# ScalarE takes the two exps of a slot ahead of the copy of its scores and of the row of maxima

## The chip, the cores and the metric

The kernel runs on one core of a Trainium2 chip. The metric is the device time in microseconds (us), the median of the runs. The engines are TensorE (PE in the profile, PEld for its weight loads), VectorE (DVE), ScalarE (ACT), GpSimd (POOL) and the queue that issues the DMAs (SP).

## The reference

A decoder layer with three parts, each added to x and followed by a layer norm: causal self-attention (32 heads of 16), cross-attention on a context of 1601 keys (32 query heads of 128, 8 key and value heads), and a mixture of 28 low-rank experts. Four batches of 256 rows of width 512. The change is in the cross-attention:

```python
q = (query @ Wq + bq).reshape(B, L, NKV, G, HDIM)
k_, v_ = jnp.split(kv @ Wkv + bkv, 2, axis=-1)
scores = jnp.einsum('blkgd,bmkd->bkglm', q, k) * scale
attn = jax.nn.softmax(scores, axis=-1)
o = jnp.einsum('bkglm,bmkd->blkgd', attn, v).reshape(B, L, NHEAD * HDIM)
return o @ Wo + bo
```

## The kernel before

The four batches run one after the other (b = 0 to 3). In each, self-attention comes first, then cross-attention, then the experts. Cross-attention is 32 heads (`NHB`; n counts them over all batches, 0 to 127). Values are held as a high and a low part, so each product is three matmuls.

**Slots.** The 1601 keys are 13 tiles of 128 (the last of 65), taken in pairs: `NSL` = 7 pairs a head, the seventh with one tile. Every engine runs the same loop, `for g in SLOTS`, and does in slot g what constants like `SCORE = -13` or `EXP = -3` say: a step with start t works at slot g on pair number g - t, counted through all heads of the batch. `slot_of` gives the (head, pair) of a step done for every pair; `head_of` that of a step done once a head. Nothing else sets the order: within a slot each engine's order is that of its code, and an engine waits at an instruction until its semaphores are there, with all behind it. Below, "slot s of head n" is the slot that weighs pair s of head n (`VALUE = 0`). In it run:

- PE: `scores` of the pair 13 further on (six matmuls into one of two banks; three where the pair is the short one, in slot 0), in slot 3 `spread_maxima` of the next head (L1151), in slot 6 `spread_reciprocals` (L1232), then the jobs of the slot, then `weigh` of pair s (six matmuls into dn; three in slot 6), in slot 1 `turn_maxima` of the next head (L1143), in slot 5 `sum_rows` (the matmuls sp<-cst,sua).
- ACT: in slot 0 `take_heads_sum` of the head just weighed (orw, L713), `keep_scores` (the copy kept_s from the scores' bank, L684, short form L682), in slot 3 `keep_max` of the next head (mrow, L692), `exponentials` of the pair 3 further on (ph, L702, into SBUF, and the same once more into a PSUM bank, sp, L705), then `job_high`, the high part of each job's result.
- DVE: `job_low` of the jobs of the slot before, `low_and_sum` of the pair 2 further on (pl, L904, and its sum: sua, L910, or L907, which for the first pair of a head starts the sum again), in slot 2 `row_maxima` (L893), in slot 5 `row_reciprocals` (L917), in slot 0 `normalize` (L924), then `maximum` of the pair 13 further on (mxa, L886, for the short pair L883).
- POOL: `shift_scores` of the pair 4 further on (L524, kept_s minus mrow), in slot 1 `finish_head` (L536 to L540); in the first batch also three splits of weight pieces a head (L514, L516), in slots 0, 2 and 4.

**Jobs** are the projections, in the two banks of a ring: for keys (K, twelve matmuls of 400 columns), queries (Q, twelve of 256), values (V, twelve of 256) and output (O, six of 512). Counted in a batch: heads 0 to 28 have a Q job in slot 2. Heads 7, 15, 23 have V jobs in slots 1 to 6, and the heads behind these (8, 16, 24) in slots 0 to 4. Heads 1, 5, ..., 25 have K jobs in slots 4 to 6 and heads 2, 6, ..., 26 one in slot 1. O jobs are in slots 3 and 5 of heads 3, 11, 19, 27; slots 5 and 6 of heads 4, 6, 12, 14, 20, 22, 28, 30; slots 1 and 3 of heads 9, 17, 25. So heads 0, 2, 10, 18, 26 and 29 have no job in slots 3 to 6.

**Waits that matter here.** `scores` waits for the copy (cp_ok) and the maximum (mx_ok) of the pair two before, which used its bank. The maximum waits for the copy (cp_ok). `shift_scores` waits for mrow (mr_ok) and the copy of its own pair, made nine slots earlier. The first exp waits for `shift_scores` (sb_ok) and for the weighing of the slot before (pv_mm), since ph has four places. The second also waits for DVE's sum in the slot before (su_ok), since its two banks are read there. L907 waits for `sum_rows` of the head before (sx_mm). `weigh` of a head's first pair waits for orw of the head before (oc_ok), since dn is one bank. `turn_maxima` waits for L883 (mx_ok).

Of the kernel before, what the change touches and what calls it, by code (L numbers as in the profile page):

```python
# [73 lines left out]
SCORE, SHIFT, EXP, LOW, VALUE = -13, -4, -3, -2, 0  # L74
# [4 lines left out]
def slot_of(g, start):  # L79

    h, s = divmod(g - start, NSL)
    return [(h, s)] if 0 <= h < NHB else []


def head_of(g, start):

    h, s = divmod(g - start, NSL)
    return [h] if s == 0 and 0 <= h < NHB else []
# [101 lines left out]
def build(nc, x, x_t, ctx_t, ws, wso, wk_in, wv_in, wq_in, wo_in, bo_s, bo_x, wb, wga, wlb, rope, consts, wk2, wv2, wq2, wo2, out, nb=B):  # L190
    with ExitStack() as ctx:
# [376 lines left out]
        def _(act):  # L568
# [18 lines left out]
            for b in range(nb):  # L587
# [63 lines left out]
                def job_high(kind, p, i):  # L651

                    act.wait_ge(job, jobs_to(b, kind, p, i))
                    src = ring_bank(b, kind, p, i)
                    done = (job_hi, 1)
                    if kind == "K":
                        kv, j = divmod(i, len(KCH))
                        a, n = KCH[j]
                        if b or p or kv:
                            act.wait_ge(sc_mm, (b * NHB + p * NHD + kv * G - 1) * NSL + last_slot_of(j) + 1)  # L660
                        nc.scalar.activation(kh[:, a:a + n], src[:, 0:n], ACT.Identity,
                                             bias=cst[:, 2 * p + C_BK + kv:2 * p + C_BK + kv + 1]).then_inc(*done)
                    elif kind == "Q":
                        h = p * NHD + i
                        if b * NHB + h >= G:
                            act.wait_ge(sc_mm, (b * NHB + h - G + 1) * NSL)
                        nc.scalar.activation(qh[:, h % G, :], src[:, 0:S], ACT.Identity,
                                             bias=cst[:, C_BQ + h:C_BQ + h + 1]).then_inc(*done)
                    elif kind == "V":
                        n = LAST if i == KT - 1 else P  # L670
                        if b or p:
                            act.wait_ge(pv_mm, (b * NHB + p * NHD - 1) * NSL + i // 2 + 1)
                        nc.scalar.activation(vh[0:n, i, :], src[0:n, 0:2 * P], ACT.Copy).then_inc(*done)

                def keep_scores(h, s):

                    n = b * NHB + h
                    k = n * NSL + s
                    src, dst = sbank[k % 2], kept_s[:, n % 2, 2 * s:2 * s + len(KEYS[s]), :].rearrange("p t q -> p (t q)")
                    act.wait_ge(sc_mm, k + 1)  # L680
                    if s == NSL - 1:
                        nc.scalar.activation(dst, src[:, 0:S], ACT.Identity, bias=cst[:, C_TAIL:C_TAIL + 1]).then_inc(cp_ok, 1)  # L682
                    else:
                        nc.scalar.activation(dst, src[:, :], ACT.Copy).then_inc(cp_ok, 1)  # L684

                def keep_max(h):

                    n = b * NHB + h
                    act.wait_ge(mr_mm, n + 1)
                    if n >= 2:  # L690
                        act.wait_ge(sb_ok, (n - 1) * NSL)
                    nc.scalar.activation(mrow[:, n % 2, :], mbank[:, 0:S], ACT.Copy).then_inc(mr_ok, 1)  # L692

                def exponentials(h, s):

                    n = b * NHB + h
                    k, cols = n * NSL + s, S * len(KEYS[s])
                    src = kept_s[:, n % 2, 2 * s:2 * s + len(KEYS[s]), :].rearrange("p t q -> p (t q)")
                    act.wait_ge(sb_ok, k + 1)
                    if k >= PH:  # L700
                        act.wait_ge(pv_mm, k - PH + 1)
                    nc.scalar.activation(ph[:, k % PH, 0:cols], src, ACT.Exp, scale=XSCALE).then_inc(ph_ok, 1)  # L702
                    if k >= 2:
                        act.wait_ge(su_ok, k - 1)
                    nc.scalar.activation(pbank[k % 2][:, 0:cols], src, ACT.Exp, scale=XSCALE).then_inc(pr_ok, 1)  # L705

                def take_heads_sum(h):

                    n = b * NHB + h
                    act.wait_ge(pv_mm, (n + 1) * NSL)  # L710
                    if n >= 2:
                        act.wait_ge(ot_ok, n)
                    nc.scalar.activation(orw[:, n % 2, :], dn[:, 0:S], ACT.Copy).then_inc(oc_ok, 1)  # L713
# [8 lines left out]
                for g in SLOTS:  # L722
                    for h in head_of(g, HEAD_SUM):
                        take_heads_sum(h)
                    for h, s in slot_of(g, SCORE):
                        keep_scores(h, s)
                    for h in head_of(g, MAX_ROW):
                        keep_max(h)
                    for h, s in slot_of(g, EXP):
                        exponentials(h, s)  # L730
                    for j in JOBS[g]:
                        if j[0] != "O":
                            job_high(*j)
# [620 lines left out]
```

## Time and profile before

| | us |
|---|---|
| median of 3 runs | 3050.05 |
| lowest, highest | 3045.78, 3051.54 |
| the profiled execution | 3042.88 |
| its span | 3041.1 |
| PE busy | 2831.5 (93%) |
| DVE busy | 2171.2 (71%) |
| ACT busy | 1906.0 (63%) |
| POOL busy | 1570.0 (52%) |

The numbers of one profile stand against its own time, 3042.88 us. A row of the time line has its start in us from the span's start, its duration in us, engine, line and operation, what it writes and reads, and in brackets the idle time of its engine ahead of it and what ended that. ACT's and DVE's operations overlap by about 0.1 us. A busy share is an average over stages with different limits. The cross-attention of the four batches lies at about 125 to 745, 890 to 1496, 1641 to 2247 and 2392 to 2998 us.

### The profile page before, as it was taken

How to read it: one execution, taken by the hardware profiler on the slowest of the kernel's cores; microseconds unless marked ns; L12 is line 12 of the kernel's file. 1: busy time of each engine (PE TensorE's matmuls, PEld its weight loads, DVE VectorE, ACT ScalarE, POOL GpSimd, SP SyncE). 2: the span in 40 equal slices, each digit the busy share in tenths (PEclk: the TensorE clock that was granted, in tenths of full speed). 3: DMA queues.
4: the chain of work that ended last, by engine and by line, in shares of the span. 5: the costliest groups of instructions: out<-in, count | busy, mean ns of one | idle time of the engine just before them, and what ended most of it. 6: DMA issues, size and time to landing. Idle time of an engine off the chain costs nothing.

```text
span 3041.1 us, 60253 instructions
## 1 busy us (share of the span) xinstructions
PE 2831.5 (93%) x20784; PEld 2619.2 (86%) x20784; DVE 2171.2 (71%) x4492; ACT 1906.0 (63%) x4264; POOL 1570.0 (52%) x1535
## 2 busy tenths in 40 slices
PE   7899999998899999999889999999978999999996
PEld 6789999997689999999668999999967899999985
DVE  5587777777558777777665877777756587878785
ACT  4476666665557666666565766666646576666663
POOL 4288787755125555555511645454542254555553
PEclk9999999998999999999899999999989999999998
DMA  5356564513311112121321112121222121212112
GB/s 186 134 190 208 165 215 162 178 50 115 103 42 56 70 64 77 63 77 63 121 89 43 65 62 77 64 77 56 80 111 89 36 84 42 97 43 91 50 53 97
DMA packets 97915, 285.08 MB, mean 94 GB/s; under 512 B 9936, under 2 KB 18256, under 8 KB 94416
## 3 DMA queue, kind: packets, MB, share of 16 engines
q1 hardware_dynamic: 97616, 281.24, 27.1%
q8 instruction: 170, 2.79, 0.4%
q14 instruction: 129, 1.06, 0.1%
HBM read 237.16 MB, written 44.04 MB: 92 GB/s over the span
## 4 chain that ended last, share of the span: by engine, by line
PE 78%; issue 7%; ACT 6%; POOL 3%; DVE 3%; DMA 2%; DVEq 0%; SPq 0%; ACTq 0%; POOLq 0%
PE bank L1012 41%; PE dn L1012 18%; PE sp L1012 14%; PE sp L1143 2%; ACT ph L702 2%; POOL kept_s L524 1%; ACT orw L713 1%; PE sp L1232 1%; PE sp L1083 1%; PE sp L1151 1%; ACT pn L629 1%; POOL lob L516 1%; DVE nmx L819 1%; POOL orw L536 0%; DMA wqk<-in_ws 0%
## 5 line engine op out<-in xcount | busy, mean ns | idle before, releaser
L524 POOL TENSOR_TENSOR kept_s<-kept_s,mrow 128x512 f32<-128x512 f32 (+1 forms) x896 | 1061.1, 1214 | 539.8 <-ACT mrow L692 539.8
L904 DVE TENSOR_TENSOR pl<-sp,ph 128x512 fp32r<-128x512 f32 (+1 forms) x896 | 577.0, 644 | 43.3 <-ACT sp L705 42.8
L702 ACT ACTIVATE ph<-kept_s 128x512 fp32r<-128x512 f32 (+1 forms) x896 | 534.8, 597 | 35.1 <-POOL kept_s L524 30.3
L1012 PE MATMUL dn<-ph,vh 128*128 128x256 f32 (+1 forms) x1664 | 492.5, 296 | 59.6 <-ACT orw L713 54.9
L705 ACT ACTIVATE sp<-kept_s 128x512 f32<-128x512 f32 (+1 forms) x896 | 506.3, 565 | 3.5 <-DVE sua L910 2.2
L910 DVE TENSOR_TENSOR sua<-sp,sua 128x512 f32<-128x512 f32 (+1 forms) x768 | 487.7, 635 | 0.0
L1012 PE MATMUL dn<-ph,vl 128*128 128x256 f32 (+1 forms) x1664 | 470.5, 283 | 0.0
L1012 PE MATMUL dn<-pl,vh 128*128 128x256 f32 (+1 forms) x1664 | 469.2, 282 | 0.0
L684 ACT ACTIVATE kept_s<-bank 128x512 f32<-128x512 f32 x384 | 229.0, 596 | 330.6 <-PE bank L1012 330.6
L1012 PEld LDWEIGHTS dn<-ph,vh 128*128 128x128 f32 (+1 forms) x1664 | 314.5, 189 | 95.2 <-ACT orw L713 86.6
L684 ACT ACTIVATE kept_s<-sp 128x512 f32<-128x512 f32 x384 | 229.6, 598 | 254.8 <-PE sp L1012 254.8
L536 POOL TENSOR_SCALAR orw<-orw,cst 128x256 f32<-128x256 f32 x128 | 118.3, 925 | 459.2 <-DVE orw L924 459.2
L1012 PEld LDWEIGHTS dn<-pl,vh 128*128 128x128 f32 (+1 forms) x1664 | 315.3, 189 | 5.6
L1012 PEld LDWEIGHTS dn<-ph,vl 128*128 128x128 f32 (+1 forms) x1664 | 315.3, 189 | 0.0
L1012 PE MATMUL bank<-wvx,ctxh 128*128 128x256 f32 (+1 forms) x1664 | 305.6, 282 | 0.0
L1012 PE MATMUL bank<-ctxh,wk 128*128 128x400 f32 (+1 forms) x1024 | 292.5, 348 | 3.1 <-DVE xres L843 3.1
L1012 PE MATMUL bank<-qh,kh 128*128 128x256 f32 (+1 forms) x832 | 245.2, 295 | 10.1 <-DVE ql L864 5.2
L1012 PEld LDWEIGHTS bank<-wvx,ctxh 128*128 128x128 f32 (+1 forms) x1664 | 251.2, 184 | 0.0
L907 DVE COPY sua<-sp 128x512 f32<-128x512 f32 x128 | 88.5, 691 | 223.8 <-PE sp L1012 223.8
L1012 PE MATMUL sp<-qh,kh 128*128 128x256 f32 (+1 forms) x832 | 243.2, 292 | 0.2
L1012 PE MATMUL bank<-wvx,ctxl 128*128 128x256 f32 (+1 forms) x832 | 233.7, 281 | 0.0
L1012 PE MATMUL sp<-qh,kl 128*128 128x256 f32 (+1 forms) x832 | 232.9, 280 | 0.0
(147 smaller groups left out, 7009.0 us busy)
## 6 DMA issues: line engine op xcount, KB each, us to landing
wqx<-wq SPq DMA_DIRECT2D x128, 512.0 KB, 3.4
wox<-wo SPq DMA_DIRECT2D x64, 1024.0 KB, 4.9
wk<-wk SPq DMA_DIRECT2D x32, 512.0 KB, 4.5
wvx<-wv SPq DMA_DIRECT2D x16, 1024.0 KB, 5.8
raw<-in_ctx_t SPq DMA_DIRECT2D x48, 200.0 KB, 2.5
wqk<-in_ws SPq DMA_DIRECT2D x17, 513.0 KB, 3.9
raw<-in_wq_in SPq DMA_DIRECT2D x32, 256.0 KB, 3.8
wq<-hib SPq DMA_DIRECT2D x32, 256.0 KB, 2.0
```

The source lines that it names most:

```text
L516: nc.gpsimd.tensor_tensor(lob[:, :], raw[:, r % 2, :], hib[:, :], ALU.subtract).then_inc(raw_free, 1)
L524: nc.gpsimd.tensor_tensor(kept_s[:, n % 2, i:z, :], kept_s[:, n % 2, i:z, :], mrow[:, n % 2, :].unsqueeze(1).broadcast_to([P, z - i, S]), ...
L536: nc.gpsimd.tensor_scalar(o, o, bias, None, ALU.add).then_inc(oh_ok, 1)
L629: nc.scalar.activation(pn[:, n % 3, a:z], s_bank[n % 5][:, a:z], ACT.Exp, bias=nmx[:, n % 3, qb:qb + 1], accum_out=sm[:, n % 3, qb:qb + 1] ...
L684: nc.scalar.activation(dst, src[:, :], ACT.Copy).then_inc(cp_ok, 1)
L702: nc.scalar.activation(ph[:, k % PH, 0:cols], src, ACT.Exp, scale=XSCALE).then_inc(ph_ok, 1)
L705: nc.scalar.activation(pbank[k % 2][:, 0:cols], src, ACT.Exp, scale=XSCALE).then_inc(pr_ok, 1)
L904: nc.vector.tensor_tensor(pl[:, k % PH, 0:cols], src, ph[:, k % PH, 0:cols], ALU.subtract).then_inc(pl_ok, 1)
L907: nc.vector.tensor_copy(sua[:, 0:cols], src).then_inc(su_ok, 1)
L910: nc.vector.tensor_tensor(sua[:, 0:cols], src, sua[:, 0:cols], ALU.add).then_inc(su_ok, 1)
L1012: return nc.tensor.matmul(dst, lhs, rhs, start=first, stop=final)
L1143: last = nc.tensor.transpose(mbank[:, col:col + P], mxa[:, e * S + tb * P:e * S + (tb + 1) * P], ident)
```

## The change

In ACT's loop the call of `exponentials` goes from behind `keep_scores` and `keep_max` to the place ahead of them. `take_heads_sum` stays first and `job_high` last.

```diff
                 for g in SLOTS:
                     for h in head_of(g, HEAD_SUM):
                         take_heads_sum(h)
+                    for h, s in slot_of(g, EXP):
+                        exponentials(h, s)
                     for h, s in slot_of(g, SCORE):
                         keep_scores(h, s)
                     for h in head_of(g, MAX_ROW):
                         keep_max(h)
-                    for h, s in slot_of(g, EXP):
-                        exponentials(h, s)
                     for j in JOBS[g]:
                         if j[0] != "O":
                             job_high(*j)
```

PE, DVE, POOL and SP keep their instructions in the same order; ACT has as many as before.

ACT, slots 3 to 5 of a head without a job there (head 2 of the first batch), before. The copies of the scores are kept_s, mrow is the row of maxima, ph and sp4<-kept_s are the two exps:

```order
L684 ACTIVATE kept_s<-bank2 128x512 [waits sc_mm]
L692 ACTIVATE mrow<-sp4 128x256 [waits sb_ok,mr_mm]
L702 ACTIVATE ph<-kept_s 128x256 [waits pv_mm,sb_ok]
L705 ACTIVATE sp4<-kept_s 128x256 [waits su_ok]
L684 ACTIVATE kept_s<-sp4 128x512 [waits sc_mm]
L702 ACTIVATE ph<-kept_s 128x512 [waits pv_mm,sb_ok]
L705 ACTIVATE sp4<-kept_s 128x512 [waits su_ok]
L684 ACTIVATE kept_s<-bank2 128x512 [waits sc_mm]
L702 ACTIVATE ph<-kept_s 128x512 [waits pv_mm,sb_ok]
L705 ACTIVATE sp4<-kept_s 128x512 [waits su_ok]
```

The same place in the changed kernel:

```order
L702 ACTIVATE ph<-kept_s 128x256 [waits pv_mm,sb_ok]
L705 ACTIVATE sp4<-kept_s 128x256 [waits su_ok]
L684 ACTIVATE kept_s<-bank2 128x512 [waits sc_mm]
L692 ACTIVATE mrow<-sp4 128x256 [waits sb_ok,mr_mm]
L702 ACTIVATE ph<-kept_s 128x512 [waits pv_mm,sb_ok]
L705 ACTIVATE sp4<-kept_s 128x512 [waits su_ok]
L684 ACTIVATE kept_s<-sp4 128x512 [waits sc_mm]
L702 ACTIVATE ph<-kept_s 128x512 [waits pv_mm,sb_ok]
L705 ACTIVATE sp4<-kept_s 128x512 [waits su_ok]
L684 ACTIVATE kept_s<-bank2 128x512 [waits sc_mm]
```

The short exps went ahead of mrow; the exps that need POOL's subtraction of mrow follow it directly, and the copy of slot 4 follows them.

ACT, slot 6 of the same head and slot 0 of the next, before (orw is the copy of the head's sum):

```order
L684 ACTIVATE kept_s<-sp4 128x512 [waits sc_mm]
L702 ACTIVATE ph<-kept_s 128x512 [waits pv_mm,sb_ok]
L705 ACTIVATE sp4<-kept_s 128x512 [waits su_ok]
L713 ACTIVATE orw<-dn 128x256 [waits ot_ok,pv_mm]
L682 ACTIVATE kept_s<-bank2,cst 128x256 [waits sc_mm]
```

And in the changed kernel:

```order
L702 ACTIVATE ph<-kept_s 128x512 [waits pv_mm,sb_ok]
L705 ACTIVATE sp4<-kept_s 128x512 [waits su_ok]
L684 ACTIVATE kept_s<-sp4 128x512 [waits sc_mm]
L713 ACTIVATE orw<-dn 128x256 [waits ot_ok,pv_mm]
L702 ACTIVATE ph<-kept_s 128x512 [waits pv_mm,sb_ok]
```

The copy now stands last ahead of orw, and the exps of slot 0 directly behind orw.

## Rows read from the trace of the kernel before

**Rows 1.** The page's first part: busy time, share of the span, instructions.

```profile
PE 2831.5 (93%) x20784; PEld 2619.2 (86%) x20784; DVE 2171.2 (71%) x4492; ACT 1906.0 (63%) x4264; POOL 1570.0 (52%) x1535
```

**Rows 2.** Busy us (instructions) of PE, PEld, DVE, ACT, POOL by stretch; clock; DMA.

```profile
1641.00:2247.00 606.00, 583.22 (x4446) 556.23 (x4444) 465.60 (x870) 405.05 (x841) 327.49 (x317) 1.00 0.20 70
```

**Rows 3.** Waits, whole span: who waited for whom, us in total, times, longest.

```profile
POOL kept_s L524 <- ACT mrow L692: 539.8, 118, 26.3
...
DVE sua L907 <- PE sp L1012: 223.8, 123, 3.2
...
PE dn L1012 <- ACT orw L713: 54.9, 85, 1.8
...
PE sp L1143 <- DVE mxa L883: 10.2, 33, 0.6
```

**Rows 4.** Time line of ACT, slots 3 and 4 of head 82 (head 18 of its batch).

```profile
2016.10 0.60 ACT L684 ACTIVATE kept_s<-bank 128x512 f32<-128x512 f32 x1 [0.83 <-PE bank L1012]
2016.60 0.38 ACT L692 ACTIVATE mrow<-sp 128x256 f32<-128x256 f32 x1
2016.86 0.42 ACT L702 ACTIVATE ph<-kept_s 128x256 fp32r<-128x256 f32 x1
2017.17 0.39 ACT L705 ACTIVATE sp<-kept_s 128x256 f32<-128x256 f32 x1
2017.74 0.60 ACT L684 ACTIVATE kept_s<-sp 128x512 f32<-128x512 f32 x1 [0.18 <-PE sp L1012]
2018.39 0.64 ACT L702 ACTIVATE ph<-kept_s 128x512 fp32r<-128x512 f32 x1
2018.93 0.58 ACT L705 ACTIVATE sp<-kept_s 128x512 f32<-128x512 f32 x1
```

**Rows 5.** Time line of POOL, the same place.

```profile
2017.05 3.79 POOL L524 TENSOR_TENSOR kept_s<-kept_s,mrow 128x512 f32<-128x512 f32 x3 [4.69 <-ACT mrow L692]
```

**Rows 6.** Time line of DVE and PE, head 82's slot 5 to head 83's slot 1.

```profile
2020.64 0.69 DVE L907 COPY sua<-sp 128x512 f32<-128x512 f32 x1 [0.41 <-PE sp L1012]
...
2025.24 0.41 DVE L883 TENSOR_TENSOR mxa<-bank,mxa 65x256 f32<-65x256 f32 x1
...
2025.70 0.55 PE L1143 MATMUL sp<-cst,mxa 128*128 128x128 f32 x3
```

**Rows 7.** Time line of all engines, change from head 80 to head 81.

```profile
1981.00 0.28 PE L1012 MATMUL dn<-pl,vh 128*128 128x256 f32 x1
1981.12 0.28 PE L1012 MATMUL dn<-ph,vl 128*128 128x256 f32 x1
...
1982.22 0.69 DVE L907 COPY sua<-sp 128x512 f32<-128x512 f32 x1 [1.37 <-PE sp L1012]
...
1983.53 0.62 ACT L702 ACTIVATE ph<-kept_s 128x512 fp32r<-128x512 f32 x1
...
1984.57 0.37 ACT L713 ACTIVATE orw<-dn 128x256 f32<-128x256 f32 x1
1984.69 0.68 DVE L886 TENSOR_TENSOR mxa<-sp,mxa 128x512 f32<-128x512 f32 x1
...
1985.00 0.38 PE L1012 MATMUL dn<-ph,vh 128*128 128x256 f32 x1 [0.78 <-ACT orw L713]
...
1986.82 0.41 DVE L883 TENSOR_TENSOR mxa<-bank,mxa 65x256 f32<-65x256 f32 x1
...
1988.63 0.60 PE L1143 MATMUL sp<-cst,mxa 128*128 128x128 f32 x4
```

**Rows 8.** Time line of ACT, slot 6 of head 2, first batch.

```profile
206.60 0.63 ACT L702 ACTIVATE ph<-kept_s 128x512 fp32r<-128x512 f32 x1 [0.75 <-POOL kept_s L524]
```

**Rows 9.** Time line of ACT, the first exp of the third batch.

```profile
1657.34 0.60 ACT L684 ACTIVATE kept_s<-bank 128x512 f32<-128x512 f32 x1 [0.33 <-PE bank L1012]
1657.96 1.28 ACT L702 ACT_TABLE_LOAD   x1
1659.25 0.64 ACT L702 ACTIVATE ph<-kept_s 128x512 fp32r<-128x512 f32 x1
```

## The prediction

> **What bounds the kernel now.** Read first the page's busy times and the table of windows [rows 1, 2]: TensorE (PE) is busy 93% of the span, and in the attention stretch of a later batch 583 of 606 us at full clock. So 1 us on PE's path is 1 us of the time, and what PE doesn't wait for is free. Then read the waits [rows 3]: the largest of PE's is for ScalarE's (ACT's) copy of a head's sum, orw L713: 54.9 us in 85 places. The second that matters here is for VectorE's (DVE's) last maximum of a head, mxa L883: 10.2 us in 33. The third thing to see there is GpSimd (POOL): it stands still 539.8 us until ACT has written mrow L692. At last read the time lines of two kinds of head [rows 4 to 7] and two single places [rows 8, 9].
>
> Slots are counted as in the text ahead: slot s of a head is the one that weighs its pair s.
>
> **What the change moves.** Nothing is added or taken out. ACT's exps go ahead of the copy and of mrow in every slot. The exps of slot g wait for POOL's subtraction, for the weighing of slot g-1 and (the second) for DVE's sum of slot g-1. The copy waits for the scores of slot g. The next operation starts 0.52 us after an exp and 0.50 us after a copy [rows 4, 7]. Two exps are 1.04 us against some 0.7 us from the end of a weighing to the end of the next scores (six matmuls, 0.12 us apart [rows 7]), so an undisturbed copy comes about 0.35 us later than now and the exps 0.7 us earlier. Who wants the copy? DVE's maximum, and the scores two slots on: 2.8 us or more later, so 0.35 us is hidden. Three places are left where it isn't so.
>
> **1. The slot after mrow (loss).** POOL can subtract only when mrow is there: in the head shown, mrow starts at 2016.60, POOL at 2017.05, and the first exp at 2018.39 [rows 4, 5]. Now the copy of slot 4 runs inside this wait, at 2017.74. Changed, it stands behind both exps: 2018.39 + 0.54 + 0.52 = 2019.45, which is 1.71 us later, and takes 0.60, to 2020.05. Does mrow itself move? Before it two exps of 256 columns now stand (0.31 us each, [rows 4]); they may start when the weighing of slot 2 ends and the 0.70 us of slot 3's scores cover their 0.62, so mrow stays where it is, by a margin of under 0.1 us.
> DVE takes the late copy first and then the rest in its fixed order: maximum 2020.08 to 2020.68, pl, and L907 from 2021.28 instead of 2020.64 [rows 6]. That is +0.64 us. PE's scores of slot 6 wait for that maximum (+0.3), the reciprocals' turn L1232 for DVE's L917 (+0.64). From L907 to L883 DVE has no gap: L907, L917, maximum, pl, sum, maximum, pl, sum, L924, L883. It ends now at 2025.65, PE's turn L1143 starts at 2025.70 [rows 6]: PE waits for it, so the 0.64 us reach the end of the kernel.
> Where does this hold? Where slots 3, 4 and 5 have no job for PE, so that DVE and PE are back at L907 before the delay is used up: heads 0, 2, 10, 18 and 26 of each batch. In the other heads an O, K or V job of 1.4 us or more (6 to 12 matmuls) lies between, and DVE waits for PE at L907 longer than 0.64 us. Head 29 has no job either, but DVE is behind there already: some 0.2 us. Sum: 5 x 0.62 + 0.2 = 3.3 us a batch; in the first batch POOL sets the pace around head 18 (below), and I take 2.7 + 0.5.
>
> **2. The change of heads (gain, mostly covered).** orw must be copied before PE may weigh the next head. Now it stands behind slot 6's copy and exps: in the second head shown the exps run from 1983.53 on, orw at 1984.57, PE goes on at 1985.00 after 0.78 us of waiting [rows 7]. Changed: the first exp at 1981.5, when the weighing that ends with the matmul at 1981.12 is done; the second waits for L907, which starts at 1982.22 and takes 0.69, so it runs at 1982.96; copy at 1983.48; orw at 1983.97. orw is 0.60 us earlier. (In the nearest simple count, the two exps gone from ahead of orw, it would be 0.66, down to the floor of the places where ACT isn't late.) There are 13 such places in a later batch and 8 in the first, each with the same 0.78 us.
> But what is late next? In 9 of 13 it is L883: the turn waits for DVE's gapless chain from L907, which is timed by PE's sums in slot 5 and not by orw. The first head shown is one: the turn starts 0.05 us after L883 ends [rows 6]. There the gain is 0. It remains where slot 1 has a job and DVE is done early: L883 at 1986.82, turn at 1988.63 [rows 7]. These are the changes into heads 9, 17 and 25, three a batch. Even there the next scores wait for the maximum that starts at 1984.69 [rows 7] and ends 0.68 later: 0.41 us of 0.60 are left. Gain 3 x 0.41 = 1.2 us a batch. The last place, in the batch's tail, is covered by DVE too.
>
> **3. Where POOL is late (loss).** In the first batch POOL splits the weights as well, and exps wait for it in front of orw: at 206.60 the exp of slot 6 starts after a wait of 0.75 us for POOL, and the copy has been made before it [rows 8]. Changed, the copy stands between exps and orw: +0.5 us on orw. These places are the changes into heads 1, 3, 11 and 19 to 21. The first three are heads of part 1, where the same 0.6 us of DVE's delay run beside this, so it isn't added; 19 to 21 are paced by POOL's own dense work, and 0.5 us is added once. That is the 0.5 above.
>
> **4. The table load.** ACT loads its table once a batch just ahead of the first exp, 1.28 us, and the exp starts 0.01 us after it ends [rows 9]. It now follows a copy that waited for PE; changed, it starts about 1 us earlier and falls into POOL's subtraction. What follows is timed by DVE: gain 0.1 us at most, taken as 0. The Trainium skill ("ScalarE: Activation LUTs", What ACT_TABLE_LOAD costs) gives the load 1283 ns, as here, and a drain of 1380 ns behind it. By that the chain would be some 0.4 us later a batch, an estimate from the page; the row shows no such drain.
>
> **The sum.** Later batches: 3.3 - 1.2 = +2.1 us each, 6.3 for three. First batch: 3.2 - 1.2 = +2.0. Together +8.3, taken as +8. The profiled execution took 3042.88 us (span 3041.1), so it would take 3050.9. It lies 7.2 us under the median of the runs shown, 3050.05; on that the forecast is **3058 us**, 0.26% slower. Bounds of my own sum: if each part-1 place costs 0.5 and the gain is the full 0.60, +4.5; if the gain is nothing and each place costs the 0.69 of a whole DVE instruction, +14.
>
> **Rivals.**
> A, the head changes pay in full (faster): if L883 isn't what the turn really waits for, or DVE's chain starts earlier with the exps, 47 places give 0.60 us: -28 us, 3022. For it speaks that orw is PE's largest wait [rows 3]; against it the 0.05 us between L883 and the turn. The Trainium skill ("Perfetto Trace Analysis", Optimization Strategies) advises to optimize the engines that keep matmuls waiting, which read on rows 3 is this rival; it says nothing of a second wait just behind.
> B, the two halves cancel (no change): DVE makes up the 0.64 us in part 1, say because pl or the maximum can run in the time in which it now waits for PE's sums. Then only the gain of 1.2 a batch is left: -5 to +4 us, 3045 to 3054. For it: DVE's waits for L907 are long in most heads (223.8 us in 123 places [rows 3]). Against: in the heads of part 1 there are just 0.4 us of it.
> C, mrow slips too (slower): the margin ahead of mrow is under 0.1 us. If the short exps aren't done when slot 3's scores are, mrow, POOL and the next exps slip by up to their 0.62 us in every head with few jobs. With some 22 such places on PE's path that is +14 on top: +22, 3072. It decides as soon as the weighing of slot 2 or DVE's sum of slot 2 ends later than now against the scores. The worst form of it is the first batch, where the exps ahead of mrow may wait for POOL, whose next work waits for mrow.
>
> **Chances.** Forecast 0.52, A 0.08, B 0.26, C 0.14. What a measurement can tell from no change is about 0.2%, 6.1 us; the forecast lies little above it, so of its 0.52 I give 0.36 to slower and 0.16 to the same. Slower 0.36 + 0.14 = 0.50, the same 0.16 + 0.26 = 0.42, faster 0.08. The range takes in B and the better part of C, and leaves A and C's worst out: 3044 to 3072.
>
> **What would show it.** In the changed kernel: (1) in heads 2, 10, 18, 26 and 0 the copy L684 of slot 4 starts some 1.06 us after an exp that waited for POOL, L907 no longer starts with the end of PE's sums but behind a pl, 0.6 us later, and these heads are longer by 0.6 us; (2) PE's wait for orw falls from 54.9 to about 25 us, while its wait for L883 grows from 10.2 by about as much as fell at the covered places; (3) heads 9, 17 and 25 begin 0.6 us earlier after their sums and keep 0.4; (4) POOL's start against mrow, and mrow against slot 3's scores, are unchanged. If mrow starts later than 0.5 us after the copy of slot 3 did, or if the copy of slot 3 waits behind short exps, C is at work. If L883 ends well ahead of the turn in heads 3 and 4, A is. The forecast falls as a whole if heads with jobs in slots 3 to 5 change their length too.

## The result

| | before | changed |
|---|---|---|
| median, us | 3050.05 | 3063.87 |
| lowest, highest | 3045.78, 3054.75 | 3063.12, 3067.60 |
| the profiled execution | 3042.88 | 3067.60 |
| its span | 3041.1 | 3065.8 |

The changed kernel takes 1.0049 times the time of before (95% interval 1.0034 to 1.0063), 10 to 19 us more. The forecast was 3058.0 us, range 3044 to 3072: slower, as forecast, and more than forecast. A second comparison of the same two kernels gave 1.0050 (1.0033 to 1.0067). Two executions in a slow state, one of 3960.02 us of the kernel with the change everywhere but in slot 4 and one of 6586.19 us of that with slot 6 alone, are in no median or ratio below.

The profile of the changed kernel answers to [rows 1] with this line: ScalarE (ACT) and VectorE (DVE) do the same instructions, TensorE (PE) is busy 25 us longer with the same 20784 matmuls.

```profile
PE 2856.9 (93%) x20784; PEld 2635.8 (86%) x20784; DVE 2154.2 (70%) x4492; ACT 1939.8 (63%) x4264; POOL 1571.4 (51%) x1535
```

Its waits, whole span (who waited for whom, us in total, times, longest), to be read against [rows 3]:

```profile
POOL kept_s L524 <- ACT mrow L692: 542.9, 124, 26.3
...
DVE mxa L886 <- ACT kept_s L684: 211.3, 160, 4.4
...
DVE sua L907 <- PE sp L1012: 193.0, 100, 3.2
...
PEld sp L1143 <- DVE mxa L883: 27.8, 56, 1.4
...
PE dn L1012 <- ACT orw L713: 22.8, 84, 1.5
...
PE sp L1143 <- DVE mxa L883: 15.0, 46, 1.2
...
PE sp L1232 <- DVE rs L917: 11.2, 32, 0.9
```

Several of them bear on the question. PE's wait for orw fell from 54.9 to 22.8 us, by 32 us. That didn't reach the end, and not all of it is orw being earlier: with the change in slot 4 alone, which leaves orw's place as it was, the wait falls to 46.6 us too (the two other profiles of the kernel before have 52.7), while PE waits longer at other places. DVE's wait for its copy grew from 46.1 to 211.3 us (most of it idle that costs nothing). PE's wait for L883 grew by 4.8 us, that of its weight loads (PEld) for the same L883 by 9.2 (18.6 before), and PE's for the reciprocals L917 by 5.9 (5.3 before). One more has no name. PE's own waits show it, here of the changed kernel; in the kernel before it is 4.3 us, 3 times:

```profile
PE bank L1012 <- issue: 19.2, 25, 1.4
```

**The slot after mrow.** The changed kernel's head 82 starts 13.71 us later than that of before (2021.20 against 2007.49). The time line from slot 3 to the turn in slot 1 of the next head, all engines, against [rows 4 to 6]:

```profile
2030.31 0.38 ACT L692 ACTIVATE mrow<-sp 128x256 f32<-128x256 f32 x1
...
2030.77 7.51 POOL L524 TENSOR_TENSOR kept_s<-kept_s,mrow 128x512 f32<-128x512 f32 x6 [4.69 <-ACT mrow L692]
...
2032.09 0.63 ACT L702 ACTIVATE ph<-kept_s 128x512 fp32r<-128x512 f32 x1 [1.40 <-POOL kept_s L524]
2032.62 0.58 ACT L705 ACTIVATE sp<-kept_s 128x512 f32<-128x512 f32 x1
2033.14 0.58 ACT L684 ACTIVATE kept_s<-sp 128x512 f32<-128x512 f32 x1
...
2033.76 0.69 DVE L886 TENSOR_TENSOR mxa<-sp,mxa 128x512 f32<-128x512 f32 x1 [1.91 <-ACT kept_s L684]
...
2034.96 0.68 DVE L907 COPY sua<-sp 128x512 f32<-128x512 f32 x1
...
2039.54 0.41 DVE L883 TENSOR_TENSOR mxa<-bank,mxa 65x256 f32<-65x256 f32 x1
...
2040.01 0.66 PE L1143 MATMUL sp<-cst,mxa 128*128 128x128 f32 x4 [0.17 <-DVE mxa L883]
```

Less 13.71, mrow and POOL stand at 2016.60 and 2017.06, where they were. The copy stands at 2019.43, which is 1.69 us later; L907 at 2021.25 (+0.61), L883 at 2025.83 (+0.59), the turn at 2026.30 (+0.60).

**A change of heads with orw early.** Head 80 to head 81, all engines, against [rows 7]; here the offset is 13.99 us:

```profile
1996.21 0.69 DVE L907 COPY sua<-sp 128x512 f32<-128x512 f32 x1 [1.49 <-PE sp L1012]
...
1996.94 0.60 ACT L705 ACTIVATE sp<-kept_s 128x512 f32<-128x512 f32 x1 [0.71 <-DVE sua L907]
...
1997.48 0.58 ACT L684 ACTIVATE kept_s<-sp 128x512 f32<-128x512 f32 x1
...
1997.96 0.37 ACT L713 ACTIVATE orw<-dn 128x256 f32<-128x256 f32 x1
...
1998.38 0.39 PE L1012 MATMUL dn<-ph,vh 128*128 128x256 f32 x1 [0.17 <-ACT orw L713]
...
1998.68 0.68 DVE L886 TENSOR_TENSOR mxa<-sp,mxa 128x512 f32<-128x512 f32 x1
...
1999.46 0.36 PE L1012 MATMUL sp<-qh,kh 128*128 128x256 f32 x1
```

Less 13.99, orw starts at 1983.97 and PE goes on at 1984.39, 0.61 earlier than before. The maximum L886 stays at 1984.69. The scores that wait for it start 0.10 us after its end, 0.34 earlier than before, and their first step is 0.20 us instead of 0.12: some 0.27 us are left.

**Where orw's 0.61 us goes to nothing.** Head 84 (local head 20), DVE and PE of the changed kernel:

```profile
2053.73 0.39 PE L1012 MATMUL dn<-ph,vh 128*128 128x256 f32 x1 [0.17 <-ACT orw L713]
...
2054.63 0.68 DVE L886 TENSOR_TENSOR mxa<-bank,mxa 128x512 f32<-128x512 f32 x1
...
2055.41 0.36 PE L1012 MATMUL bank<-qh,kh 128*128 128x256 f32 x1 [0.70 <-issue]
```

PE is let go by orw after 0.17 us, weighs, and stands 0.70 us in front of the scores, which start 0.10 us after the maximum L886 ends. The trace calls this wait "issue". In the kernel before, the same maximum starts at 2040.32, the scores at 2041.11: both have moved by 14.3 us. So the wait for orw became a wait for L886, at a place that the table of waits gives to nobody. That the scores start just behind L886, and wait for it in the code, is what names it; the trace itself gives no releaser, and no experiment moved L886 alone.

### The profile page after: what moved, and what is told of

It is laid out like the page before. It is cut to its first block, busy times and chain, and to the rows that moved or that the text cites. A ratio compares the mean times of both kernels' runs of the same rounds, so it can differ in the third digit from the quotient of the medians.

```text
span 3065.8 us, 60253 instructions
## 1 busy us (share of the span) xinstructions
PE 2856.9 (93%) x20784; PEld 2635.8 (86%) x20784; DVE 2154.2 (70%) x4492; ACT 1939.8 (63%) x4264; POOL 1571.4 (51%) x1535
## 4 chain that ended last, share of the span: by engine, by line
PE 67%; issue 14%; DVE 9%; POOL 4%; ACT 4%; DMA 1%; DVEq 0%; SPq 0%; ACTq 0%; POOLq 0%
PE bank L1012 36%; PE dn L1012 14%; PE sp L1012 11%; POOL kept_s L524 2%; DVE sua L910 2%; PE sp L1143 2%; DVE pl L904 1%; DVE mxa L886 1%; PE sp L1232 1%; PE sp L1083 1%; ACT pn L629 1%; PE sp L1151 1%; POOL orw L536 1%; DVE mxa L883 1%; ACT kept_s L684 1%
## 5 line engine op out<-in xcount | busy, mean ns | idle before, releaser
L1012 PE MATMUL dn<-ph,vh 128*128 128x256 f32 (+1 forms) x1664 | 495.5, 298 | 27.6 <-ACT orw L713 22.8
L1012 PE MATMUL bank<-qh,kh 128*128 128x256 f32 (+1 forms) x832 | 245.6, 295 | 20.4 <-issue 14.9
L886 DVE TENSOR_TENSOR mxa<-sp,mxa 128x512 f32<-128x512 f32 x256 | 174.2, 680 | 109.8 <-ACT kept_s L684 109.7
L886 DVE TENSOR_TENSOR mxa<-bank,mxa 128x512 f32<-128x512 f32 x256 | 174.1, 680 | 96.9 <-ACT kept_s L684 96.7
L1012 PE MATMUL sp<-ql,kh 128*128 128x256 f32 (+1 forms) x832 | 233.5, 281 | 0.0
```

What stands on the lines that cost most here:

```text
L886: nc.vector.tensor_tensor(mxa[:, 0:cols], sbank[k % 2][:, 0:cols], last, ALU.max).then_inc(mx_ok, 1)
L1012: return nc.tensor.matmul(dst, lhs, rhs, start=first, stop=final)
```

## The experiments

The kernels from here on have a condition for the place of `exponentials`; with `exps_first` always true it is the change. Only the condition is shown of each. The line numbers behind ScalarE's loop are 5 higher in these kernels, so L1148 is the turn that was L1143 and L888 the maximum that was L883.

```diff
+                    exps_first = g % NSL != 4
+                    if exps_first:
+                        for h, s in slot_of(g, EXP):
+                            exponentials(h, s)
                     for h, s in slot_of(g, SCORE):
                         keep_scores(h, s)
                     for h in head_of(g, MAX_ROW):
                         keep_max(h)
-                    for h, s in slot_of(g, EXP):
-                        exponentials(h, s)
+                    if not exps_first:
+                        for h, s in slot_of(g, EXP):
+                            exponentials(h, s)
```

"Heads 0 to 28" and "tail" (heads 29 and 30) below are the difference, from the starts of the heads' first weighing matmuls in two traces, between how long these heads last in a kernel and in the kernel before.

### Everywhere but in slot 4

> The change is kept in every slot but slot 4 (the one behind the row of maxima), which has the old order: copy, then exps. Theory 1 (the loss is the copy of slot 4, held behind exps that wait for POOL): the +0.60 us in slot 6 of heads 0, 2, 10, 18, 26 goes, five times a batch, and with it the three falls of the granted clock in the first batch (at 213, 370, 527 us of the changed kernel) and those in the tails of the later batches. What stays is the gain of some 0.3 us in heads 9, 17, 25: 3 to 8 us under the kernel before. Theory 2 (the later copy of every slot is to blame: DVE's wait for the copy is 211 us instead of 46): taking one slot in seven out gives back a seventh, so still 10 us or more slower than before.

Measured: 3055.02 us, 1.0017 (1.0005 to 1.0028). The expected loss of slot 4 is gone: heads 0 to 28 are 0.78, 0.51 and 0.89 us shorter in the three later batches. But the kernel isn't faster: the tail is longer by 2.7, 0 and 1.3 us, and the first batch by 4.1, where the clock falls at heads 1, 3, 11 and 19 (the runs of the kernel before, below, show that most of these 4.1 us come and go with the execution). The mechanism was there, its sign in the total was missed, and the falls, which were expected to go, stayed.

### Slot 4 alone

```diff
+                    exps_first = g % NSL == 4
```

> Only slot 4 has exps first, all other slots the old order. Theory 1: the losses without the gains: +0.6 us in heads 0, 2, 10, 18, 26 of each batch, PE's wait for orw about as before, 12 us or more slower than before, plus what the clock costs. Theory 2: a seventh of the change, so 2 us slower at most.

Measured: 3057.78 us, 1.0033 (1.0023 to 1.0044). Heads 0 to 28 are 2.95, 2.95 and 2.80 us longer in the later batches: 0.60 us for each of heads 0, 2, 10, 18 and 26, where it starts in slot 6, and nothing in the heads with jobs there. The waits show the place: the scores' maximum waits for the copy nearly as long as in the changed kernel, and PE for L917 at the turn of the reciprocals (L1237 here).

```profile
DVE mxa L891 <- ACT kept_s L684: 206.2, 152, 5.5
...
PE dn L1017 <- ACT orw L713: 46.6, 84, 1.8
...
PE sp L1237 <- DVE rs L922: 12.1, 34, 0.9
```

So the later copies of the other six slots add next to nothing to DVE's wait. The first batch is another matter: its heads 0 to 28 are only 0.59 us longer, against a profile of before that, like this one, has no fall of the clock in them. Heads 1, 3, 11 and 19 show none of the loss there. The two halves add: -0.78 + 2.95 = 2.17 in batch 1, and the changed kernel has 2.13.

### Slot 6 alone

```diff
+                    exps_first = g % NSL == 6
```

> Only slot 6 has exps first. Theory 1: orw 0.6 us earlier in 13 places a batch, of which only the changes into heads 9, 17, 25 keep some 0.3 us: 3 to 5 us faster than before in all, less 0.5 us at each of the places of the first batch where an exp waits for POOL in front of orw. Theory 3 (rival A of the prediction: the head changes pay in full once slot 4 is out of the way): 0.6 us at all 47 places, 20 us or more faster.

Measured: 3052.82 us, 1.0017 (1.0005 to 1.0028). Heads 0 to 28: -0.77, -0.80, -0.91. So the whole gain of the change comes from slot 6, and is 0.8 us in a later batch. PE's wait for orw is 26.9 us, and its nameless wait 15.5 us in 19 places, with no loss of slot 4 anywhere: it comes from orw being early. The tail is 1.3, 1.2 and 2.7 us longer, which makes it slower after all. 3 to 5 us faster had been expected. In the first batch slot 6 is a loss, not a gain. PE starts heads 1, 3, 11 and 19 later by about 0.5 us each, since the copy now stands between the late exps and orw:

```profile
213.86 0.39 PE L1017 MATMUL dn<-ph,vh 128*128 128x256 f32 x1 [2.13 <-ACT orw L713]
```

This is head 3; in the kernel before its wait is 1.64 us.

### Slot 6 alone, and DVE's maximum earlier

```diff
                 # DVE
+                    late_sum = g % NSL == 0
+                    if not late_sum:
+                        for h, s in slot_of(g, LOW):
+                            low_and_sum(h, s)
...
                         if s:
                             maximum(h, s)
+                    if late_sum:
+                        for h, s in slot_of(g, LOW):
+                            low_and_sum(h, s)
```

> Exps first in slot 6 alone, and in slot 0 DVE takes L924 and the maximum L883 ahead of pl and sua, so that L883 ends up to 1.2 us earlier. If the turn's wait for L883 is what covers the gain of the head changes, it now shows: the turn's waits (4.7 us a batch before) go, heads 3, 11, 19, 27 get 0.3 us or more from the earlier orw, and the kernel is 15 to 28 us faster than before. If the turn waits for something else, it is no faster than with slot 6 alone.

Measured: 3035.54 us, 0.9959 (0.9945 to 0.9974). With L883 moved forward, heads 0 to 28 of a later batch are 6.2 to 6.4 us shorter. The cover named in the prediction is real. The tails of the three later batches are 1.5 us longer each, with a fall of the clock. How much of the gain is DVE's alone, the next one tells.

### DVE's maximum earlier, ScalarE as before

```diff
+                    exps_first = False
```

(and DVE's order as in the last one)

> ScalarE's order as before; VectorE takes, in slot 0 of a head, the normalisation and the maximum L883 ahead of the low part and its sum (1.36 us earlier). Theory 1 (two waits one behind the other at the change of heads: orw first, L883 just behind): alone this pays only what TensorE's turn waits for L883 today, at most the 10.2 us of the wait in the trace of the kernel before, so 2 to 9 us faster. Together with the kernel that has the exps first in slot 6 alone (which was 5 us slower) the two edits would give 4 us faster at most if they simply added, and 14.5 us faster were measured for both in one kernel: theory 1 expects them not to add. Rival (the gain of that kernel came from VectorE's order alone): 14 us faster or more.

Measured: 3033.61 us, 0.9961 (0.9946 to 0.9977), 7 to 16 us faster. The bound of 10.2 us that was set for it is broken: heads 0 to 28 are 4.07, 4.09 and 4.16 us shorter, 12.3 us in the three batches, and some 3.5 in the first if the fall of the clock in head 3 is left out (that in head 19 is given back). The cause is a row that was read too narrowly. PE's wait for L883 is 10.2 us, but the turn's weight load waits for the same instruction, and that row of the kernel before is larger:

```profile
PEld sp L1143 <- DVE mxa L883: 18.6, 38, 0.8
```

With DVE's maximum early both rows are gone. Both edits together, in the kernel above, save 6.2 to 6.4 us a batch where they would give 0.8 + 4.1 = 4.9 if they only added. So about 1.3 us a batch of orw's gain had been behind L883. Even then only some 2.1 us of the 13 x 0.60 = 7.8 a batch come through; at heads 4, 12, 20 and 28 the maximum L886 still stops PE. The larger part of what the fourth kernel gained was DVE's own. The rival was nearer here than the theory. In the tails of the kernel with DVE's edit alone the turn no longer waits; PE has one idle stretch of 2.4 us at the spread of the maxima there, where the kernel before has two, of 0.6 and 1.6.

### The old order in the first batch

```diff
+                    exps_first = b > 0
```

> Exps first in the three later batches, the old order in the first. Theory 1 (the time is the sum of what the heads lose, place by place): the attention of the first batch lost 4.8 us in the changed kernel, of it 3.6 us behind falls of the granted clock in heads 3, 11 and 19; undone, the kernel is 8 to 11 us slower than before instead of 14, and no clock fall stands in those heads. Rival (falls of the clock there come with the run and not with the order): 13 to 15 us slower, falls in the first batch as before the undoing.

Measured: 3063.99 us, 1.0052 (1.0034 to 1.0071), no better than the changed kernel. The first batch has three falls of the granted clock, in heads 3, 11 and 19, though its order is the old one. The theory that the change makes them is out. In its profile the first batch's cross-attention is 3.3 us shorter than in the changed kernel (1.5 in heads 0 to 28, 1.8 in the tail), and the work ahead of it 2.2 us longer; that the medians show nothing of the 3.3 was not followed up.

### The old order in the last three heads

```diff
+                    exps_first = g < NSL * 29
```

> Exps first in heads 0 to 28 of each batch, the old order in the last three heads. Theory 1: the changed kernel lost 0.3, 1.9, 3.2 and 3.1 us in heads 29 and 30 of the four batches, because ScalarE's order there lengthens the idle stretches of TensorE and the granted clock halves; undone, about 8 us of the 14 come back: 4 to 8 us slower than before. Rival (a fall of the clock there comes with the run, since the kernel before has one in its first batch): 12 to 15 us slower.

Measured: 3061.17 us, 1.0044 (1.0027 to 1.0062), 13 us slower and so the rival's number. The tail is 0.0, 1.37, 1.36 and 1.34 us longer than in the profile of before instead of 0.3, 1.9, 3.2 and 3.1, which is 4.5 us less; 8 had been expected. What is left is a fall of the clock in head 30 in each batch.

### The kernel before, and the changed one, again

> The kernel before, once more. Theory 2 (falls of the granted clock behind the same idle stretches come with the run and not with ScalarE's order): the places inside the slots are the same to 0.02 us, but the falls stand elsewhere than at 726.6 us: some of heads 3, 11, 19 of the first batch and head 30 of any batch have one (1.5 and 1.4 us each) that had none, and the span is 2 to 8 us longer than 3041.1. Theory 1 (the order decides where they fall): falls at the same places, span within 1 us.

> The changed kernel, once more. Both theories: heads 0 to 28 of the later batches 2.0 to 2.5 us longer than in the kernel before. Theory 2: one or more of the seven falls in heads 3, 11, 19 of the first batch and head 30 of the four is missing or has another length. Theory 1: all seven again, with the lengths 3.4 us (first batch, second batch) and 6.8 us (last two).

Measured: before again, 3048.37 us, 0.9993 (0.9982 to 1.0005), span 3046.8; the changed one again, 3066.27 us, 1.0050 (1.0033 to 1.0067). In its later batches heads 0 to 28 of the kernel before last as long as in its first profile, to 0.2 us. In the first batch it now has falls in heads 3, 11 and 19 that the first profile had not, and one more at head 1. Those at heads 1, 3 and 11 cost 1.5 us each; that of head 19 shows as 0.5 us at the start of head 20 and is given back by head 22. No tail has one. They come at the end of one idle stretch of 1.6 us, in which PE waits for orw. The kernel's first profile has the same stretch without a fall, here at head 3, the second profile behind it:

```profile
208.07 0.39 PE L1012 MATMUL dn<-ph,vh 128*128 128x256 f32 x1 [1.64 <-ACT orw L713]
```

```profile
210.41 0.58 PE L1012 MATMUL dn<-ph,vh 128*128 128x256 f32 x1 [1.63 <-ACT orw L713]
```

The windows of the clock, for the first profile of before and for its second (stretch, busy us and count of PE, PEld, DVE, ACT and POOL, granted clock, DMA share, GB/s); the first:

```profile
209.60:213.00 3.40, 3.40 (x32) 3.40 (x31) 2.87 (x6) 2.96 (x6) 3.33 (x3) 1.00 0.83 307
```

and the second:

```profile
210.41:213.82 3.41, 3.41 (x16) 3.41 (x17) 2.82 (x6) 1.76 (x4) 3.33 (x4) 0.50 0.86 304
367.40:370.80 3.40, 3.40 (x17) 3.40 (x18) 2.68 (x6) 1.86 (x5) 3.32 (x4) 0.50 0.62 218
524.40:527.80 3.40, 3.40 (x18) 3.40 (x18) 2.54 (x6) 1.99 (x5) 3.32 (x4) 0.50 0.53 202
```

PE shows busy throughout in both, but does 16 matmuls in the place of 32: the clock is at 1.2 instead of 2.4 GHz. So a comparison of two single profiles of this kernel says nothing of its first batch. Of the changed kernel, all seven falls in heads 0 to 30 are there again; that of the third batch's tail lasts 3.4 instead of 6.8 us, and the tail is 1.5 us shorter.

### The kernel before a third time, and the old tail again

> The kernel before, a third time. If a fall of the clock in head 30 (1.4 us) came by chance alone, with the chance that all profiles so far show (most tails with the new order in the heads ahead of them have it, 1 of 8 tails of the kernel before), 0 to 1 of the four tails here has one, and heads 29 and 30 last 27.0 us together without it, 28.5 with it. Falls in heads 3, 11, 19 of the first batch: as in the second profile of this kernel (three, 1.5 us each), or none as in the first; either says that the order doesn't decide.

> Exps first in heads 0 to 28, the old order in the last three heads, a second time. In the first profile all four tails had a fall of the clock in head 30, with idle stretches of TensorE that are those of the kernel before (0.6, 1.6, 0.9 us). Theory 2 (it comes with the run): at least one tail is without it, 27.0 instead of 28.4 us for heads 29 and 30. Rival (the order in the heads ahead decides, by the moment at which the tail begins): all four again.

Measured: 3049.88 us and 3066.69 us, one run each. The kernel before has three falls in heads 3, 11 and 19 once more, and no tail with one. The kernel with the old tail has them in the tails of the three later batches and not in the first. Here is its PE in the third batch's tail, the turn and the spread of the maxima; the fall starts at 2248.81, while PE still stands in the second idle stretch:

```profile
2246.03 0.65 PE L1148 MATMUL sp<-cst,mxa 128*128 128x128 f32 x4 [0.59 <-DVE mxa L888]
...
2249.02 0.69 PE L1156 MATMUL sp<-cst,mcol 128*128 128x128 f32 x2 [1.62 <-DVE mcol L898]
```

The same place in the third profile of the kernel before:

```profile
2234.56 0.65 PE L1143 MATMUL sp<-cst,mxa 128*128 128x128 f32 x4 [0.58 <-DVE mxa L883]
...
2237.55 0.43 PE L1151 MATMUL sp<-cst,mcol 128*128 128x128 f32 x2 [1.62 <-DVE mcol L893]
```

The idle times are equal; only the two matmuls behind them, 0.69 against 0.43 us, tell that the clock has fallen in the one. And the changed kernel, where the first of the two idle stretches is twice as long:

```profile
2242.07 0.66 PE L1143 MATMUL sp<-cst,mxa 128*128 128x128 f32 x4 [1.19 <-DVE mxa L883]
...
2245.06 0.69 PE L1151 MATMUL sp<-cst,mcol 128*128 128x128 f32 x2 [1.62 <-DVE mcol L893]
```

The windows of these falls, old tail and changed kernel (each a view of its own); the old tail:

```profile
2248.81:2252.20 3.39, 3.18 (x15) 3.18 (x16) 2.11 (x5) 1.64 (x5) 1.99 (x2) 0.50 0.01 2
```

the changed kernel:

```profile
2244.20:2251.00 6.80, 5.94 (x22) 5.36 (x23) 3.35 (x7) 3.31 (x7) 5.22 (x5) 0.50 0.00 1
```

Counted over the profiles:

| heads ahead of the tail | order in the tail | tails with a fall |
|---|---|---|
| before (3 profiles) | before | 1 of 12 |
| changed (2 profiles) | before | 7 of 8 |
| DVE's maximum early (2 profiles) | exps as before | 0 of 8 |
| changed (2 profiles) | changed | 8 of 8, three of them 6.8 us long |

The third line is the kernel with DVE's maximum early and ScalarE as before, and the last kernel below; only the second of the two has the idle stretches of before in its tails. Not in the table: the kernels with slot 4, slot 6 or all but slot 4 changed and the one with slot 6 and DVE's maximum, whose tails have parts of the new order, had falls in 2, 3, 2 and 3 of 4 tails, and the one with the old first batch in none with the old order and in all three with the new. In the kernel with slot 4 alone the later tails begin 2.8 to 2.95 us later after their batch's first head, and two of the three have no fall. Heads 29 and 30 last 27.0 us together without a fall, 28.4 with one, 28.7 to 28.9 in the changed order, and 30.2 with the long one. So neither side of the last test holds as it was put. The falls don't follow from the order in the tail, and they aren't blind chance either: with the same idle stretches they come behind the heads of the changed kernel (all six tails of the later batches) and not behind those of before (none of nine). What differs there is when the tail begins, 1.9 to 2.6 us later after its batch's first head. That alone doesn't decide it either, as the kernel with slot 4 alone shows. What does decide it is open; no experiment moved the moment alone.

### The version that the experiments point to

```diff
+                    exps_first = b > 0 and g % NSL == 6 and g < NSL * 29
...
+                    late_sum = g % NSL == 0 and g < NSL * 29
```

> Exps first in slot 6 alone, in batches 1 to 3 and heads 0 to 28; VectorE's normalisation and L883 ahead of its low part and sum in slot 0 of heads 0 to 28. Theory 1: 6.2 us less in each later batch (as in the kernel with both edits everywhere), nothing lost in the last heads, some 1 to 2 us less in the first batch: 18 to 22 us faster than before, 3027 to 3032. Rival (the loss in the last heads comes from being earlier and stays): 12 to 16 us faster.

Measured: 3026.60 us, 0.9934 (0.9910 to 0.9959), 12 to 27 us faster than before. Heads 0 to 28 are 6.10, 6.11 and 6.25 us shorter in the later batches, the tails equal to before's, and none has a fall. Theory 1 expected 3027 to 3032, the rival 3032 or more. It is the fastest here, though its interval overlaps those of the two with DVE's maximum early.

## Why the prediction was right, and what it missed

A profile of before that has the same falls in the first batch is the fair partner: the third one, 3049.88 us. Against it the changed kernel's profiled execution, the slowest of its five, is 17.7 us longer; the medians differ by 13.8. By place, in us:

| batch | heads 0 to 28 | heads 29, 30 |
|---|---|---|
| first | +1.4 | +1.8 |
| second | +2.2 | +1.9 |
| third | +2.5 | +3.2 |
| fourth | +2.2 | +3.2 |
| sum | +8.3 | +10.1 |

The rest of the span gives back 0.7. In the changed kernel's second profile the same two sums are 8.6 and 8.6.

**The heads, right in the later batches.** The sum forecast for heads 0 to 28 was some 7.5 us (8.3 less 0.2 for each head 29); they measure 8.3. Forecast for a later batch were 3.1 lost and 1.2 gained; slot 4 alone loses 2.8 to 2.95, slot 6 alone gains 0.8 to 0.9. Part 1 was right to the step there: copy 1.71 us later forecast, 1.69 measured; L907 and the turn 0.64 forecast, 0.61 and 0.60 measured; in just the five heads named; slot 4 alone shows it by itself.

**mrow, right.** It stands 9.11 us after its head's start in both kernels, so rival C is out, though the margin was small.

**The change of heads, right in kind, wrong in two sizes.** orw was forecast at 1983.97 and is there to the hundredth. Of its 0.60 us, 0.27 and not 0.41 stay in heads 9, 17 and 25: the row of the waiting scores has a start 0.10 us behind its releaser and a first step longer by 0.08 us, which the step left out. And where the gain is covered, it isn't always by L883: at heads 4, 12, 20 and 28 the maximum L886, of the same gapless chain of DVE, stops PE in slot 0 already. The step named one waiting instruction where two stand in a row. Rival A had its largest argument in [rows 3], and lost: with slot 6 alone the wait for orw is 26.9 us instead of 54.9, and heads 0 to 28 of a later batch are 0.8 us shorter. The forecast that PE's wait for L883 would grow by about as much as the other fell at the covered places was half right: it grew by 4.8 us in PE's row and by 9.2 in that of its weight loads, and 14.9 us went to "issue". That PE's wait for orw came out near the 25 us forecast is luck in part: 6 to 8 us of its fall are there with slot 4 alone, which moves nothing in front of orw.

**The tail, missed.** This is the step that failed: "Head 29 has no job either, but DVE is behind there already: some 0.2 us", and for the last change of heads "covered by DVE too". The place itself costs 0.5 us (slot 6 of head 29), not 0.2. The rest of the 10.1 us is a halved clock behind the idle stretches in head 30: about 1.4 us in each tail that has a short fall, 2.7 in those with a long one. In three profiles of the kernel before it struck one tail of twelve. The prediction took the clock for full throughout the attention because [rows 2] showed 1.00, and asked nowhere whether it could fall. The 1.19 us in front of the turn, 0.61 more than before, stand just ahead of the 1.62; but the old tail shows that falls of 1.4 us come without them. The long falls are seen only in tails that have the new order or a part of it. So the forecast's +8 and the measured +14 lie close by luck in part: the prediction has no term for the clock.

**The base and the bounds.** The prediction sized its sum by a profile 7.2 us under the median and then added it to the median. That was right. The third profile's span is 7.0 us longer than the first one's: 6.1 us of it lie ahead of the first attention stretch, 3.0 come from the falls in heads 3, 11 and 19, and the first profile's one tail with a fall takes 1.5 off. None of it is the kernel's. The lower bound of its sum, given as +4.5, is +3.6 by the terms it names (0.9 for each of four batches); range and chances don't hang on it.

**The first batch, right by luck.** Its heads lost 1.4 us against 2.0 forecast, but two misses cancel. Part 1 was to cost 2.7 us there and costs 0.6 (slot 4 alone). Part 3's copy between exps and orw costs what it was said to, 0.5 us, but at each of heads 1, 3, 11 and 19, and not once: slot 6 alone makes the first batch's heads some 1.3 us longer, where part 3 less the gain of part 2 would make them 0.7 shorter. (The 1.3 is an estimate: they are 0.2 us shorter than in the third profile of before, which has one fall of 1.5 us more.) Here the step that failed is that at the first three "the same 0.6 us of DVE's delay run beside this, so it isn't added": slot 4 alone shows no such delay there. Why it isn't there was not followed up.

## What to carry over

Where one engine is let go by two others in turn, read the time line past the first wait to the next one before crediting it; a gapless chain on the second engine takes back the whole of what the first gives, and the tables may book the new wait under "issue" or under the weight load and not under the matmul. Moving the second one first was worth more here (0.9961 alone; 0.9959 with the first, and 0.9934 with both kept out of the last heads and the first out of the first batch) than the edit that went at the largest wait. A wait that shrinks is not a gain by itself: PE's wait for orw shrank by 6 to 8 us in a kernel that was slower (slot 4 alone). And where TensorE has its longest idle stretches, at the end of a stage and here in the first batch, the granted clock may fall in one execution and not in the next; take more than one profile of the kernel before to know which falls are its own.

## What was not expected of the hardware

The clock granted to TensorE falls to half (0.50, 1.2 GHz) for 3.4 or 6.8 us inside a stretch in which it is full otherwise: in the tails at idle times of 0.6 and 1.6 us some 3 us apart, in heads 3 and 11 of the first batch at a single one of 1.64 us. A short fall costs 1.4 to 1.5 us (at head 19 nothing is left of it), a long one 2.7. With the same program and the same idle times it is there in some executions and not in others (heads 3, 11 and 19: in none, all and all of three profiles of one kernel). The Trainium skill ("Perfetto Trace Analysis", Optimization Strategies) advises to optimize those engines that are "blocking the critical path" when the matmul engine waits for others. The traces show how the largest wait can mislead there: it went from 54.9 to 22.8 us, and the time didn't follow.
